# Another order for the instruction queues where the dense part of a two-layer block gives over to its mixture of experts

## The reference

```python
h = layernorm(x) * (1 + ca) + sa
xn = rmsnorm(h);  g, v, d = xn @ Wg.T + bg, xn @ Wv.T + bv, xn @ Wd.T + bd
s = scan(a = 0.001 + 0.998 * sigmoid(d), in = sigmoid(g) * tanh(v))   # causal
h = h + s
h = h + (silu(rmsnorm(h) @ W_gate.T) * (rmsnorm(h) @ W_up.T)) @ W_out.T
x = x + ga * h
h2 = layernorm(x) * (1 + cb) + sb
p = softmax(h2 @ router_w);  w, idx = top_k(p, 2)                     # 8 experts
y = sum over the 2 chosen e of  w_e * ((gelu(h2 @ w1[e]) * (h2 @ v1[e])) @ w2[e])
x = x + gb * (y + bias)
```

## Time and profile before

| | us |
|---|---|
| median of 3 runs | 859.52 (858.62 to 859.77) |
| profiled execution, its own time | 861.07 |
| profiled execution, its span | 859.3 |
| PE busy | 820.2 (95%) |
| DVE, ACT, POOL busy | 556.4, 377.0, 492.9 |
| share of the chain that ended last: PE | 81% |

### The profile page before, as it was taken

The page is one execution under the profiler, slowest core; times in us unless marked ns, Lnnn a source line. Parts: engine busy times, 40 slices in busy tenths (PEclk is TensorE's granted clock), DMA queues, the critical chain, the costliest instruction groups (busy, mean ns, idle before and its releaser), DMA issues.

```text
span 859.3 us, 18981 instructions
## 1 busy us (share of the span) xinstructions
PE 820.2 (95%) x5046; PEld 727.1 (85%) x5047; DVE 556.4 (65%) x1553; ACT 377.0 (44%) x681; POOL 492.9 (57%) x458
## 2 busy tenths in 40 slices
PE   6889999999999999969999999999999999999994
PEld 3668898989888888758899999999999999999993
DVE  5768767777775849876565565655655556555552
ACT  4775656575655515433324324224243242332230
POOL 2263645778695877569644646547537475383332
PEclk9999999999999999988999999999999999999997
DMA  8031050302020261426632422523324312222221
GB/s 281 27 113 50 1 178 1 125 26 101 1 101 13 87 221 44 157 78 159 190 49 40 135 43 37 147 43 114 64 37 142 49 31 43 37 43 44 37 37 18
DMA packets 49421, 67.61 MB, mean 79 GB/s; under 512 B 4896, under 2 KB 43680, under 8 KB 49376
## 3 DMA queue, kind: packets, MB, share of 16 engines
q1 hardware_dynamic: 35712, 47.71, 17.8%
q0 software_dynamic: 13664, 19.35, 12.0%
HBM read 43.51 MB, written 23.54 MB: 78 GB/s over the span
## 4 chain that ended last, share of the span: by engine, by line
PE 81%; POOL 5%; DVE 5%; issue 3%; ACT 2%; DMA 2%; another core or an unknown queue 0%; DVEq 0%; POOLq 0%; SPq 0%; ACTq 0%
PE ps L594 23%; PE ps L595 23%; PE ps L596 23%; PE ps L757 5%; POOL routed L1906 2%; PE ps L723 2%; PE ps L695 1%; DMA out_rows<-y_moe,tok_moe 1%; PE ps L778 1%; PE ps L777 1%; PE ps L612 1%; PE ps L682 1%; PE ps L640 1%; PE ps L647 1%; PE ps L601 1%
## 5 line engine op out<-in xcount | busy, mean ns | idle before, releaser
L594 PE MATMUL ps<-split,xT_moe_hi 128*128 (+2 forms) x426 | 167.7, 394 | 0.6 <-issue 0.5
L595 PE MATMUL ps<-split,xT_moe_lo 128*128 (+2 forms) x426 | 161.3, 379 | 0.0
L596 PE MATMUL ps<-split,xT_moe_hi 128*128 (+2 forms) x426 | 160.9, 378 | 0.0
L1917 POOL TENSOR_TENSOR y_moe<-y_moe 128x256 f32<-128x256 f32 x71 | 67.3, 947 | 132.9 <-DVE y_moe L1585 132.9
L1125 ACT ACTIVATE hidT_hi<-ps 128x768 fp32r<-128x768 f32 x71 | 57.7, 813 | 158.7 <-PE ps L757 151.8
L1926 POOL DMA_INDIRECT out_rows<-y_moe,tok_moe x71 | 111.2, 1566 | 23.2 <-issue 22.5
L594 PE MATMUL ps<-split,hidT_hi 128*128 (+1 forms) x355 | 106.4, 300 | 4.0 <-issue 2.4
L1119 ACT ACTIVATE gelu_moe<-ps 128x704 f32<-128x704 f32 x71 | 53.9, 759 | 123.4 <-PE ps L596 121.3
L596 PE MATMUL ps<-split,hidT_hi 128*128 (+1 forms) x355 | 100.7, 284 | 0.0
L595 PE MATMUL ps<-split,hidT_lo 128*128 (+1 forms) x355 | 100.5, 283 | 0.0
L1585 DVE SCALAR_TENSOR_TENSOR y_moe<-ps,gate_moe,gates 128x256 f32<-128x256 f32 x142 | 62.2, 479 | 57.0 <-PE ps L778 56.8
(11 more groups left out here) (219 smaller groups left out, 1952.5 us busy)
## 6 DMA issues: line engine op xcount, KB each, us to landing
raw<-in_w SPq DMA_DIRECT2D x9, 1408.0 KB
x_moe<-routed SPq DMA_DIRECT2D x74, 132.5 KB
raw<-in_w SPq DMA_DIRECT2D x9, 640.0 KB
x_sb<-in_x SPq DMA_DIRECT2D x8, 512.0 KB, 3.8
x_again<-in_x SPq DMA_DIRECT2D x8, 512.0 KB
out_rows<-x_again SPq DMA_DIRECT2D x8, 512.0 KB
gu_raw<-in_gu_t SPq DMA_DIRECT2D x1, 1536.0 KB, 7.2
raw<-in_w SPq DMA_DIRECT2D x18, 64.0 KB
```

Of the source, the lines that this page charges most:

```text
L594: pe.matmul(dst, a_hi, b_hi, start=first, stop=False)
L595: pe.matmul(dst, a_lo, b_hi, start=False, stop=False)
L596: return pe.matmul(dst, a_hi, b_lo, start=False, stop=last)
L1917: g.tensor_tensor(y_moe[:, t.slot, 0, :], y_moe[:, t.slot, 0, :], y_moe[:, t.slot, 1, :], ALU.add)\
```

## The change

No instruction's work changes; the order of the five queues does, from block 5's choice up to tile 5. Two waits of PE are gone, and there are 7 `fill` matmuls where there were 9.

- **DVE**: `weigh(q)` and `slots(q)` stand right behind `choose(q)` and the norm of the next block, ahead of the tiles' work; `norm2_stats(7)` stands ahead of `hidT_rest(0)`; `multiply(3)` and `xT_rest(4)` ahead of `table()`; the last `split_lo` of expert 0 comes later.
- **POOL**: `result_base(6)` leaves its place ahead of `scatter(5)` and stands, with `result_base(7)`, behind `add_rows` of tile 1. `residual(7)` stands behind all of `scatter(5)`.
- **SP**: `store_base(6)` moves from ahead of the load of expert 1 to just ahead of `store_base(7)`.
- **PE**: `rank_tokens(6)` and `(7)`, both `h2_transposes(7)` and `router_logits(7)` come earlier; `table_transposes` later, within the products of tile 4.
- **ACT**: `router_exp(6)` ahead of `gelu(1)`, `router_exp(7)` ahead of `gelu(2)`; the pieces of `split_hi(0)` are spread.

```diff
@@ SP
-            store_base(NBLK - 2)
             load_weights(sp, 1, RAW_SLOT)
...
+            store_base(NBLK - 2)
             store_base(NBLK - 1)
             load_weights(sp, 2, 0)
@@ PE
             h2_transposes(6, 0)
+            h2_transposes(6, 1)
             first_products(Tile(0), PICKED, AB[2:])
-            h2_transposes(6, 1)
...
+            rank_tokens(6)
             first_products(Tile(1), PICKED, AB[2:])
             pe.wait_ge(gelu_r, 2)
-            fill(0, 3)
+            fill(0, 4)
             x_transposes(Tile(2))
             second_product(Tile(0), PICKED)
-            rank_tokens(6)
+            fill(0, 3)
+            h2_transposes(7, 0)
             hid_transposes(Tile(1))
-            first_products(Tile(2), PICKED, AB[:2])
-            pe.wait_ge(hid_r, 2)
-            fill(2, 4)
-            h2_transposes(7, 0)
-            first_products(Tile(2), PICKED, AB[2:])
             h2_transposes(7, 1)
+            first_products(Tile(2), PICKED, AB[:1])
             router_logits(7)
+            first_products(Tile(2), PICKED, AB[1:])
             x_transposes(Tile(3))
             second_product(Tile(1), PICKED)
+            rank_tokens(7)
             hid_transposes(Tile(2))
-            rank_tokens(7)
...
-            table_transposes()
-            pe.wait_ge(gelu_r, 4)
-            fill(0, 2)
             hid_transposes(Tile(3))
             first_products(Tile(4), PICKED, AB[:2])
+            table_transposes()
             first_products(Tile(4), PICKED, AB[2:])
@@ POOL
             norm2_rstd(6)
-            result_base(6)
             scatter(5, 0)
             scatter(5, 1)
             scatter(5, 2)
+            scatter(5, 3)
             residual(7)
-            scatter(5, 3)
...
             add_rows(Tile(0))
             add_rows(Tile(1))
+            result_base(6)
             result_base(7)
```

More of the change, by code:

```diff
@@ L1281, in _ @@
             hidT_split(Tile(0))
+            router_exp(6)
             gelu(Tile(1))
+            split_hi(act, 0, 0)
             xT_split(Tile(2))
-            router_exp(6)
+            h2_copy(7, 0)
             hidT_split(Tile(1))
-            split_hi(act, 0, 0)
-            split_hi(act, 0, 1)
-            h2_copy(7, 0)
             h2_copy(7, 1)
+            router_exp(7)
             gelu(Tile(2))
             xT_split(Tile(3))
-            router_exp(7)
+            split_hi(act, 0, 1)
+            hidT_split(Tile(2))
             split_hi(act, 0, 2)
-            hidT_split(Tile(2))
             gelu(Tile(3))
@@ L1780, in _ @@
             choose(5)
+            weigh(5)
+            slots(5)
             split_lo(v, PICKED, 2)
-            slots(5)
+            norm2_scale(6)
+            add_ffn(7, 0)
+            count(5)
             take_gates(Tile(0))
-            weigh(5)
-            add_ffn(7, 0)
             take_gates(Tile(1))
-            norm2_scale(6)
             add_ffn(7, 1)
-            count(5)
+            gate_xo(7)
             multiply(Tile(0))
-            gate_xo(7)
             xT_rest(Tile(1))
             choose(6)
+            norm2_stats(7)
+            slots(6)
+            weigh(6)
             hidT_rest(Tile(0))
-            norm2_stats(7)
+            norm2_centre(7)
+            norm2_scale(7)
             multiply(Tile(1))
             xT_rest(Tile(2))
[L1798 to L1801, removed]
+            count(6)
             gate_y(Tile(0))
-            count(6)
             hidT_rest(Tile(1))
+            choose(7)
             multiply(Tile(2))
-            choose(7)
             count(7)
             xT_rest(Tile(3))
-            take_gates(Tile(2))
             slots(7)
@@ L1813, in _ @@
             gate_y(Tile(1))
+            take_gates(Tile(2))
+            multiply(Tile(3))
+            xT_rest(Tile(4))
             table()
-            split_lo(v, 0, 2)
-            xT_rest(Tile(4))
-            multiply(Tile(3))
             split_lo(v, 0, 0)
+            hidT_rest(Tile(3))
             table_out()
-            hidT_rest(Tile(3))
             gate_y(Tile(2))
+            multiply(Tile(4))
             split_lo(v, 0, 1)
-            multiply(Tile(4))
             xT_rest(Tile(5))
             take_gates(Tile(3))
+            split_lo(v, 0, 2)
+            hidT_rest(Tile(4))
             gate_y(Tile(3))
             take_gates(Tile(4))
-            hidT_rest(Tile(4))
             take_gates(Tile(5))
```

## The result

The changed kernel took 870.39 us in the median of four runs (866.53, 866.61, 874.18, 877.0) against 859.19 us: 1.014 times as long, with a 95% interval of 1.0112 to 1.0169. The forecast was 855.6 us, and the range ended at 861.9: wrong in sign and outside the range. The profiled execution is the quickest of the four, with a span of 864.7 us (before: 859.3), so it shows the smaller part of the loss. (Behind PE's list of calls the lines of kernel.py number three less than in the kernel before: L1459 is `add_ffn`, L1582 `gate_y`, L1884 `result_base`.)

A forecast was written before the change was run, and what follows sets the result against it. PE, busy 95% of the span, was taken as the bound, with gains only at 343 to 411 us. Tile 6's transposes, set by tile 2's adding DMA, come 3.9 us earlier: 859.5 - 3.9 = 855.6 us, range 853.8 to 861.9.

The forecast's parts named there:

- (a): Block 5 on POOL: scatters start at 336 instead of 340.81 us, residual(7) at 347.5, 2.1 us earlier.
- (b): Block 7's norm on DVE: statistics start at about 350, norm2_scale(7) ends at 358.5 us instead of 360.7.
- (c): Block 7's choice and ranks: choose(7) begins at 365 us instead of 367.19, rank_tokens(7) stands at 369.5.
- (d): DVE's 3.89 us rank wait leaves no gap again; block 7's scatters begin at 372.3 us, 4.6 us earlier.
- Tile 3's transposes 7.3 us earlier: On PE, multiply(3) ahead of the table lets them start near 378.4 us instead of 385.69.
- 2 to 3 us ahead of `second_product(3)`: PE idles this long at tile 3's second product, waiting for gate_y(2) on DVE, near 386.3 us.
- is added: 2.4 to 3.2 us: Extra base on POOL between block 7's mark and tile 2's DMA, taken as 2.8 us; DMA issued at 398.5.
- From there to the transposes of tile 6 PE needed 14.7 us: PE's stretch from tile 5's x_transposes, kept as before; PE alone would reach tile 6 at 405.4, gaining 5.6 us.
- The list of PE's waits: Idle places on PE between 343 and 411 us: 1.82, 2.29, 1.35 and 0.28 us ahead of named transposes.
- Tile 2's DMA as the last word: Its landing at 405.8 us decides when PE starts tile 6's transposes: 407.1, 3.9 us earlier.
- block 7's routing is not earlier: Rival: block 7's scatters start at 376 or later, tile 2's DMA lands at 409.5 to 412; 859.3 to 862 us, chance 0.14.
- the clock falls in a new wait: Rival: PE waits over 3 us ahead of tile 6 for tile 2's DMA, then half clock; 861.4 us, chance 0.20.

The follow-up runs named there:

- e6: The changed kernel unaltered, profiled a second time, on the second chip: 1.0073 times the kernel before.
- g0: The changed kernel unaltered, as yardstick on the third chip: 1.0057 times the kernel before.
- e4: The kernel before with only the change's order behind block 7's weights, block 6's base and store late, first chip: 1.0105 times the kernel before.
- e7: The changed kernel with residual(7) ahead of block 5's scatters, which wait until router_logits(6) is done, second chip: 1.0116 times the kernel before.
- e8: The changed kernel with the load of expert 1's weights waiting until router_logits(6) is done, second chip: 1.0058 times the kernel before.
- h4: Same kernel as e4, repeated on the fourth chip: 1.0042 times the kernel before.
- h8: Same kernel as e8, repeated on the fourth chip: 1.0058 times the kernel before.
- e9: The kernel before, unaltered, profiled a second time on the second chip: 854.3 us.
- h1: The kernel before with only the change's GpSimd and SyncE parts, fourth chip: 1.0017 times the kernel before.
- g2: The changed kernel with block 6's base moved between block 6's last scatter and block 7's first, third chip: 854.73 us, 1.0011 times the kernel before.
- i1: g2 with hidT_rest(3), gate_y(2), table_out ahead of expert 0's first split and hidT_rest(4), gate_y(3) ahead of its last, fifth chip: 1.0081 times the kernel before.
- i2: i1 with block 7's base behind tile 3's adding instead of tile 1's, fifth chip: 1.0044 times the kernel before.

## Why the prediction was wrong, step by step

- **(a) Block 5's scatters at 336:** right, 335.99. `residual(7)`, put at 347.5, came at 348.94, held by the late signal of `ffn_out(7, 1)`.
- **(b), (c) Norm, choice, ranks:** `norm2_scale(7)` ended at 364.14 (forecast 358.5), `choose(7)` began at 372.10 (365). In e6, without late signals, these were at 356.11 and 362.04, ahead of the forecast; so the late signals, with the half clock behind the first, are what was missing from the forecast here. The wait for `hidT_rest(0)` that I put at 2 to 2.5 us was 1.07, and 1.76 in e6.
- **(d) "This gap does not come back":** failed where the forecast was measured. It came back as 5.22 and 3.56 us on DVE at other places, and block 7's mark was at 379.57, not 372.3. On the second chip it did not come, and the mark was at 369.53 against 371.84: 2.3 us earlier, half of the 4.6. So even there the kernel before, freed of its own gap of 3.89 us, took most of that gain without the change: my 4.6 contained it.
- **Tile 3's transposes 7.3 us earlier:** mechanism right, 5.5 us in e6 (375.78 against 381.25). **2 to 3 us ahead of `second_product(3)`:** 2.88, and 3.29 in e6.
- **`result_base(6)` "is added: 2.4 to 3.2 us", and "three `split_lo` on DVE hold POOL up as before":** the step that failed in every profile of the change unaltered (first profile, e6, g0), and in e4, e7, e8, h4 and h8. I priced the added base on POOL only, by what DVE does to POOL, and never by what POOL does to DVE, though the earlier trace rows had `pos_k` at 2.27 us beside one base. DVE's split went from 1.6 to over 7 us.
- **"From there to the transposes of tile 6 PE needed 14.7 us":** taken over unchanged; it was 20.7 in e6 (409.44 - 388.73), by that wait and the clock.
- **The list of PE's waits:** of the 9.4 us idle it left out 1.61 us ahead of `second_product(2)`, for `gate_y`, and 1.28 us ahead of the table's transposes. The sum has no term for either; the second was 1.57 us in the first profile of the change.
- **Tile 2's DMA as the last word ("the one that counts"):** it did not bind. It was issued at 404.14, not 398.5, and PE, held up before, came later still. It did not bind in the kernel before either when no signal was late (e9); in h1, where nothing moved on PE and DVE, it did.
- **The rivals:** "block 7's routing is not earlier" (0.14, to 862) came nearest on the first chip, and the loss went beyond its price (870.4), since the split is not in it. That the clock falls in a new wait was right as a mechanism, but behind the split, not behind the DMA.

Shown: the collision, its size (3.7 us by g2) and that parting the bases gives it back; that late signals occur for both kernels on some chips and not on others. Argued only: that late signals make the rest of the first loss (1.4% against 0.6 to 0.7%). Each chip was measured at one time alone, so what belongs to the chip and what to the time is not told apart.

## What to carry to other kernels

Price a tensor operation that is moved to another place on GpSimd twice: its time there, and the time by which VectorE's queue beside it is stretched; here a short operation of VectorE that TensorE waits for ended only behind both of two in a row. Look for an idle stretch of GpSimd that faces waiting on VectorE, not work. Where an idle gap of the profile has no instruction at its end, don't book its removal as a gain of a new order: repeat both kernels on another chip first.

## What the runs showed that I had not expected

In both first profiles and on two of the five chips of the experiments, ten or eleven signals of TensorE in a profile (six in that of the kernel before), and hardly one of another engine, reached the others up to 6.4 us behind the end of their matmuls' rows; nearly all the rest that are on record came within 0.1 us. The kernel before was at 858.8 to 859.2 us there, and at 853.6 to 854.3 us on the three chips that had none, with the same DMA pieces (pieces of 5632 bytes at 215 ns in the median, scattered rows of 4240 bytes at 181 to 184) on both. The places repeat with the order of the queues: near 315 us in all, 368 to 375 us before; 347, 372 and near 390 us in the change and in i1 and i2. All lie in stretches with scattered rows in flight, but so do many signals that are on time. The Trainium skill, page "Perfetto Trace Analysis", section "Tensor Engine Instruction (MATMUL, LD_WEIGHTS)", says that the end of a matmul's row is estimated, and that its signal is sent when PSUM has acknowledged the bytes; so a stretched write would look like this. The rows speak against this as the only cause: in the first profile of the change the signals of both halves of `h2_transposes(6)` came 0.06 us apart, though their rows end 0.43 us apart.

One thing more sets the two kinds of profile apart, whatever the order. For nearly the same instructions and DMAs the eight profiles with late signals hold 6138 to 6354 records of a semaphore's step, the twelve without 7097 to 7129. Most that are missing are steps by DMAs that landed (3584 to 3797 against 4475 to 4502), but some 60 to 80 of the 2346 steps by engines are missing too, against 0 to 4. So what is disturbed is not TensorE's signals alone, and "remote" or "issue" in such a profile can stand for a step that was not recorded. The cause stays open.
